# Attention stage: stack loads ahead of the sums' store, output weights split in four, dense last maxima, FP4 work at round ends

## The reference, cut to what matters

```python
x = x + attention(layernorm(x), Wqkv, bqkv, Wo, bo)   # x: 2 x 1024 x 512, 16 heads of 32
x = x + fp4_ffn(layernorm(x), ...)                    # weights packed as 4-bit codes
x = x + recurrence(layernorm(x), ...)
x = x + experts(layernorm(x), ...)

# attention, for batch b and head n
scores = einsum('bsnh,btnh->bnst', k, q) / sqrt(32)
scores = triu(scores) + -10000.0 * tril(ones, k=-1)
attn = softmax(scores, axis=2)
out = einsum('bnkq,bknh->bqnh', attn, v)
return out.reshape(b, s, 512) @ Wo + bo
```

## Time and profile before

| | |
|---|---|
| runs | 1803.70, 1817.19, 1809.32 us |
| median | 1809.32 us |
| span of the profiled execution | 1799.4 us |
| mean granted TensorE clock | 0.969 |
| PE busy | 1662.0 us (92%) |
| DVE busy | 1103.2 us (61%) |
| ACT busy | 703.2 us (39%) |
| POOL busy | 587.6 us (33%) |

### The profile page before, as it was taken

One profiled execution on the slowest core, in us unless ns is written; L12 is line 12 of the kernel. 1 busy time (PEld: TensorE's weight loads), 2 busy tenths in 40 slices (PEclk: granted clock), 3 DMA queues, 4 the chain that ended last, 5 costly groups with the idle time before them and its releaser, 6 DMA issues. The chain is left out here.

```text
span 1799.4 us, 22628 instructions
## 1 busy us (share of the span) xinstructions
PE 1662.0 (92%) x7201; PEld 1177.9 (65%) x7201; DVE 1103.2 (61%) x2382; ACT 703.2 (39%) x1330; POOL 587.6 (33%) x859
## 2 busy tenths in 40 slices
PE   6997899999989899999967999999699999999995
PEld 5886454555547677777755767677477777777774
DVE  5444766666736778787878567797544444444442
ACT  3211455555552455555442142212044334433442
POOL 3001333433551334444445051121133333333322
PEclk9998799999999999999988999999899999999998
DMA  7344456556623500000010031102799999999994
GB/s 253 115 141 134 139 159 156 160 161 162 164 70 108 188 1 1 1 1 1 1 59 33 0 119 51 47 21 72 254 325 354 338 357 351 345 345 350 353 354 91
DMA packets 120679, 284.83 MB, mean 158 GB/s; under 512 B 23472, under 2 KB 35248, under 8 KB 120304
## 3 DMA queue, kind: packets, MB, share of 16 engines
q1 hardware_dynamic: 106224, 247.71, 40.0%
q0 software_dynamic: 14336, 35.66, 9.0%
HBM read 224.03 MB, written 54.69 MB: 155 GB/s over the span
## 5 line engine op out<-in xcount | busy, mean ns | idle before, releaser
L897 ACT ACTIVATE probs<-bank 128x512 f32<-128x512 f32 (+3 forms) x384 | 167.6, 503 | 185.4 <-PE bank L840 183.9
L2000 POOL DMA_INDIRECT out_x<-e_y,row_out x64 | 104.0, 1626 | 316.4 <-DMA out_x<-e_y,row_out 174.1
L2035 PE MATMUL bank<-w_gate,xgt 128*128 128x352 f32 x512 | 163.7, 463 | 0.0
L2035 PE MATMUL bank<-w_up,xgt 128*128 128x352 f32 x512 | 161.9, 459 | 0.0
L2101 DVE TENSOR_TENSOR e_hidden<-e_silu,bank 128x352 f32<-128x352 f32 x64 | 33.4, 522 | 201.4 <-issue 181.6
L815 PE MATMUL bank<-k_stack,q_stack 96*128 96x512 f32 (+2 forms) x360 | 136.2, 391 | 22.2 <-DMA k_stack<-qk_parts 11.8
L1200 PE MATMUL bank<-ln_xt_hi,gu_codes 128*128 128x512 f32 x352 | 145.6, 414 | 10.8 <-DVE gate_sum L1273 5.3
L854 PE MATMUL bank<-probs,v_ones 128*64 128x512 f32 (+3 forms) x768 | 142.1, 506 | 6.7 <-POOL probs L764 6.7
L940 DVE CUSTOM_DVE_ANT_0 masked_scores<-bank,wide_mask 128x128 bf16<-128x128 f32 (+1 forms) x240 | 109.3, 482 | 63.5 <-PE bank L815 62.8
L840 PE MATMUL bank<-q_stack,k_stack 98*128 98x512 f32 (+3 forms) x384 | 141.0, 382 | 2.1 <-ACT probs L897 1.8
L764 POOL TENSOR_SCALAR_AFFINE_SELECT probs<-probs 128x128 f32<-128x128 f32 x256 | 77.9, 321 | 196.5 <-ACT probs L897 192.4
(11 more groups left out here) (261 smaller groups left out, 3842.2 us busy)
## 6 DMA issues: line engine op xcount, KB each, us to landing
w_gate<-in_w_gate SPq DMA_DIRECT2D x64, 704.0 KB, 6.7
w_up<-in_w_up SPq DMA_DIRECT2D x64, 704.0 KB, 7.8
w_down<-in_w_down SPq DMA_DIRECT2D x64, 512.0 KB, 8.7
q_stack<-qk_parts SPq DMA_DIRECT2D x96, 128.0 KB, 3.8
k_stack<-qk_parts SPq DMA_DIRECT2D x96, 128.0 KB, 4.0
w_down<-in_w_down SPq DMA_DIRECT2D x64, 192.0 KB, 10.0
qk_parts<-qk_stage_hi SPq DMA_DIRECT2D x32, 256.0 KB, 2.0
qk_parts<-qk_stage_lo SPq DMA_DIRECT2D x32, 256.0 KB, 2.3
```

The source lines that it names most:

```text
L897: act.activation(probs[u % PROBS][:, 0:cols], m.bank[EXPB[u % 3]][:, 0:cols], ACT.Exp, scale=scale).then_inc(exp_ready, 1)
L2000: pool.indirect_dma_start(out=a["out"][:, :], out_offset=bass.IndirectOffsetOnAxis(ap=row_out[e % YS][:, :], axis=0), in_=y[e % YS][:, :], ...
L2035: last = pe.matmul(m.bank[bank[e % 2]][:, 0:F], xt[e % 2][:, k, :], w[e % R][:, k, :], start=(k == 0), stop=(k == KT - 1))
```

## The change

Six edits, all in `attention_phase`:

1. SyncE's loop issues `store_inverse` and `spread_inverse` one pair later (p - 2 in place of p - 1), right behind the stack load, and no longer at the end of the iteration. Pair 14's come behind the loop.
2. GpSimd splits the output weights in four pieces of 128 x 512 (`split_wo`), two in pair 0 and two in pair 1, behind `place_v` and behind the masks of round 2. Who needs them waits for four pieces.
3. `maxima_at(p, n)` gives the full lists as before; for pair 14 one entry per unit for n below 12, and the rest (the turn) at n = 17.
4. ScalarE does the high part and the last output copy at the start of round 1, the codes at the start of round 2, the first output copy at the start of round 3.
5. VectorE does its FP4 steps behind the last unit of a round: gate-up words behind unit 5, low part behind unit 11, down words behind unit 17.
6. VectorE inverts the sums behind unit 23.

```diff
--- before.py
+++ after.py
@@ -608,6 +608,13 @@
                 first.append(("unit", q, i))
         return first
 
+    def maxima_at(p, n):
+
+        entries = maxima_of(p)
+        if p + 2 < PAIRS:
+            return entries[(U + 1) * n // U:(U + 1) * (n + 1) // U]
+        return entries[n:n + 1] if n < LEAD else entries[LEAD:] if n == TURN_AT else []
+
     place = {entry: i for i, entry in enumerate(entry for p in range(-1, PAIRS) for entry in maxima_of(p))}
     FIRST_DONE = 2 * TPC
     DIAGONAL = [n for n in range(U) if EXP_UNITS[n // 2][1] == EXP_UNITS[n // 2][0] * P]
@@ -701,7 +708,7 @@
             def spread_inverse(p):
                 sp.wait_ge(inverse_stored, 16 * (p + 1))
                 if p == 0:
-                    sp.wait_ge(wo_ready, 1)
+                    sp.wait_ge(wo_ready, KT)
                 need(sp, normalized, p // 2 - 1)
                 for j in range(2):
                     u = (2 * p + j) % 4
@@ -720,6 +727,9 @@
                 if p >= 1 and p + 2 < PAIRS:
                     sp.wait_ge(scored, U * p)
                     load(p + 2)
+                if p >= 2:
+                    store_inverse(p - 2)
+                    spread_inverse(p - 2)
                 if p >= 1:
                     dq.sync_store_down(sp, p - 1)
                     move_out(p - 1)
@@ -727,9 +737,8 @@
                     dq.sync_load_down(sp, p + 1)
                     place_max(p + 1)
                 dq.sync_store_gu(sp, p)
-                if p >= 1:
-                    store_inverse(p - 1)
-                    spread_inverse(p - 1)
+            store_inverse(PAIRS - 2)
+            spread_inverse(PAIRS - 2)
             move_out(PAIRS - 1)
             store_inverse(PAIRS - 1)
             spread_inverse(PAIRS - 1)
@@ -781,17 +790,23 @@
 
             pool.wait_ge(ones_set, 2 * SLOTS + 4)
             place_v(0)
-            pool.wait_ge(wo_loaded, 16)
-            pool.tensor_copy(wo_hi[:, :, :], wo_raw[:, :, :]).then_inc(wo_hi_ready, 1)
-            pool.wait_ge(wo_hi_ready, 1)
-            pool.tensor_tensor(wo_lo[:, :, :], wo_raw[:, :, :], wo_hi[:, :, :].bitcast(F32),
-                               ALU.subtract).then_inc(wo_ready, 1)
+            def split_wo(k):
+                pool.wait_ge(wo_loaded, 16)
+                pool.tensor_copy(wo_hi[:, k, :], wo_raw[:, k, :]).then_inc(wo_hi_ready, 1)
+                pool.wait_ge(wo_hi_ready, k + 1)
+                pool.tensor_tensor(wo_lo[:, k, :], wo_raw[:, k, :], wo_hi[:, k, :].bitcast(F32),
+                                   ALU.subtract).then_inc(wo_ready, 1)
+
             for p in range(PAIRS):
                 mask_round(p, 0)
                 mask_round(p, 1)
                 if p + 1 < PAIRS:
                     place_v(p + 1)
+                if p < 2:
+                    split_wo(2 * p)
                 mask_round(p, 2)
+                if p < 2:
+                    split_wo(2 * p + 1)
                 if p % 2 == 1 and p >= 3:
                     normalize((p - 3) // 2)
                 mask_round(p, 3)
@@ -865,19 +880,18 @@
                 exp_unit(0, n)
                 maxima(before[1 + LEAD // 2 + LEAD // 2 * n // EXP_ROUND:1 + LEAD // 2 + LEAD // 2 * (n + 1) // EXP_ROUND])
             for p in range(PAIRS):
-                ahead = maxima_of(p)
                 for r in range(ROUNDS):
                     for n in range(EXP_ROUND * r, EXP_ROUND * (r + 1)):
                         if p > 0 or r > 0:
                             exp_unit(p, n)
-                        maxima(ahead[len(ahead) * n // U:len(ahead) * (n + 1) // U])
+                        maxima(maxima_at(p, n))
                     if r >= 1:
                         value_round(p, r - 1)
                     elif p >= 1:
                         value_round(p - 1, ROUNDS - 1)
             value_round(PAIRS - 1, ROUNDS - 1)
 
-            pe.wait_ge(wo_ready, 1)
+            pe.wait_ge(wo_ready, KT)
             for t in range(NT):
                 pe.wait_ge(a_lo, t + 1)
                 need(pe, x_added, t - 2)
@@ -906,14 +920,13 @@
             for p in range(PAIRS):
                 for r in range(ROUNDS):
                     for n in range(EXP_ROUND):
-                        if n == 2 and r == 1 and p >= 1:
+                        if n == 0 and r == 1 and p >= 1:
+                            dq.scalar_hi(act, p - 1)
                             copy_out(p - 1, 1)
-                        if n == 2 and r == 3:
+                        if n == 0 and r == 2:
+                            dq.scalar_codes(act, p)
+                        if n == 0 and r == 3:
                             copy_out(p, 0)
-                        if n == 4 and r == 0 and p >= 1:
-                            dq.scalar_hi(act, p - 1)
-                        if n == 4 and r == 2:
-                            dq.scalar_codes(act, p)
                         exponential(p, EXP_ROUND * r + n)
             copy_out(PAIRS - 1, 1)
             for t in range(NT):
@@ -980,16 +993,15 @@
             maxima(maxima_of(-1))
             dq.vector_shifts(dve)
             for p in range(PAIRS):
-                ahead = maxima_of(p)
                 for n in range(U):
-                    maxima(ahead[len(ahead) * n // U:len(ahead) * (n + 1) // U])
-                    if n == 2:
+                    maxima(maxima_at(p, n))
+                    if n == EXP_ROUND - 1:
                         dq.vector_gu_bits(dve, p)
-                    if n == 6 and p >= 1:
+                    if n == 2 * EXP_ROUND - 1 and p >= 1:
                         dq.vector_lo(dve, p - 1)
-                    if n == 13:
+                    if n == 3 * EXP_ROUND - 1:
                         dq.vector_down_bits(dve, p)
-                    if n == 22 and p >= 1:
+                    if n == 4 * EXP_ROUND - 1 and p >= 1:
                         invert(p - 1)
 
             def split_attn(t):
```

## The result

Before has a median of 1810.68 us (4 runs), the changed kernel 1782.61 us (1771.64 to 1787.21, 4 runs): a ratio of 0.9845, 95% interval 0.9805 to 0.9885, so faster by 1.2 to 2.0%. The profiled execution of after is the fastest of its four.

The account below looks back on a forecast made before the run. TensorE's own work was taken to set the pace, other engines costing only its waits. Terms 6.7 + 6.8 + 4.0 + 4.0 = 21.5 us off the 1799.4 span, plus 9.9, gave 1787.8 us; own range 1781 to 1795.

Parts of the forecast that it names:

- The 9.9 us between span and median: Distance of the three runs' median, 1809.3 us, above the profiled span, 1799.4; assumed to stay the same after the change.
- The split: Pair 0: TensorE's whole wait for the masks behind GpSimd's output-weight split goes, 6.7 us, range 4.9 to 8.5.
- round ends: FP4 work moved to round ends: the low-part subtraction's 0.31 us per pair goes, 4.0 us over 13 pairs, bounds 0 and 8.
- that open question: Pair 0: whether the clock's next rise comes later or earlier against the work; up to about half of 3.72 us at stake.
- The stack loads: Loads ahead of the sums' store: the excess of pairs 4, 5, 10 and 11 goes, 6.84 us, bounds 3 and 8.
- there is no reserve: Old SyncE order: the stack's first product starts 3.8 us after the last load issue, while slower landings take 4.7.
- What pays for it: SyncE's queue: store and spread stand behind twelve loads, maxima's rows go out at 357.5 instead of 355.83; no stall taken.
- the store's landing hides behind the wait for the low parts: SyncE, mid-pair: free of landing and spread between 348.0 and 354.4, while low parts come about 352.9 anyway.
- The rival of the other side: Pair starts: maxima's rows come 3.4 us late in each of 13 pairs, 22.7 us lost, 1832; chance 0.05.
- The rival that round ends give nothing: Round ends: VectorE's work is only shifted and not caught up, so without the 4.0 us 1791.8; chance 0.15.
- Dense maxima: Pair 14: waits behind the unpacking and for the turn, and the low clock, go; 3.99 us, bounds 2 and 5.

Follow-up runs that it names:

- E2: Kernel before with only the output-weight split in four pieces; 1802.12 us, ratio 0.9981.
- E7: Changed kernel with the extra maxima entry of a full list taken at unit 17 instead of two products at unit 23; 1788.29 us, ratio 0.9871.
- E11: Changed kernel with SyncE's old order, sums' store and spread at the end of an iteration; 1805.49 us, ratio 0.9961.
- E5: Changed kernel with the low-part subtraction back behind unit 6 and the high part back at n = 4 of round 0; 1784.92 us, ratio 0.9851.
- E6: Changed kernel with the sums' store issued ahead of the stack loads, only its spread behind them; 1777.55 us, ratio 0.9819.
- E10: Changed kernel with the last 13 maxima again spread evenly over pair 14's units; 1786.09 us, ratio 0.9837.
- E9: Changed kernel with six extra 2 KB DMAs ahead of the rows of maxima in each pair; 1831.98 us, ratio 1.0129.
- E1: Kernel before with only the sums' store and spread moved one pair later, behind the stack loads; 1800.64 us, ratio 0.9959.
- E4: Kernel before with only ScalarE's and VectorE's FP4 work at round ends and the inversion behind unit 23; 1818.95 us, ratio 1.0042.
- E3: Kernel before with only pair 14's maxima one per unit and the turn at unit 17; 1805.28 us, ratio 0.9973.

## Why the prediction was right, and where it was not

The forecast was 1787.8 us and faster by over 1%; measured were 1782.6 and 1.55%. The sum of the terms was 21.5 us, the stage gave 27.8. Where the time goes was right in all four places; that the terms could be added was luck, since the working did not see which of them need each other.

The 9.9 us between span and median were read as what lies around the span. Every run on record whose span is listed is 1.7 to 1.8 us above its own span, so some 8 of the 9.9 say only that the profiled execution of before was that much shorter than the median run. After's span lies 12.7 below its median: this term is scatter and no constant.

**The split: right, 6.7 predicted, 6.9 measured (E2).** The predicted sign was there too: the first value products of after start at 189.70 (predicted about 192), without a wait. The first piece in after, GpSimd:

```profile
189.96 0.62 POOL L795 CAST wo_hi<-wo_raw 128x512 fp32r<-128x512 f32 x1 [2.62 <-DMA wo_raw<-in_wo]
190.66 1.27 POOL L797 TENSOR_TENSOR wo_lo<-wo_raw,wo_hi 128x512 fp32r<-128x512 f32 x1
```

The same copy in before:

```profile
191.76 1.89 POOL L785 CAST wo_hi<-wo_raw 128x2048 fp32r<-128x2048 f32 x1 [15.81 <-DMA wo_raw<-in_wo]
```

So the masks of before stood behind the arrival of the weights, for which GpSimd idled 15.81 us, and not only behind the split that the working names; the change takes the masks out from behind both. A piece takes 1.9 us (estimated under 2.2), and no mask behind one is waited for. Pair 0 gained 2.3 us more than this term. About 0.8 is the unpacking's move, which takes away a wait for a maximum (1.45 us in E2): E7 and E11 have that move, and like E2 a clock of 0.50 until 16 us into the pair, and their pair 0 takes 27.4 against E2's 28.2. It is a gain of the round ends in pair 0 that the prediction overlooked, since it took pair 7 for all pairs. The rest, 1.5, goes with the clock: in after, E5, E6 and E10 it was at 1.00 for one stretch of 3.4 us around 183 and rose for good at 191 to 193 (pair 0 25.8 to 25.9), in E7, E9 and E11 it stayed at 0.50 until 194 to 195 (26.5 to 27.4). The prediction named that open question (range 4.9 to 8.5); what makes the clock rise earlier in one kernel was not found out and stays open.

**The stack loads: right in size and cause (E1), wrong as a term that stands by itself.** 6.84 us of stalls were predicted to go, and all of them go. The step that failed is that the four terms were summed as if each kept its value whatever the others do. The working said of the old order "there is no reserve", and did not draw from it that the 0.31 us per pair of the next term needs the reserve, nor that the later inversion starts the chain later: E4 shows 4.0 predicted becoming a loss of some 8, E11 the same with everything else in. The sum was near only because all parts were applied. SyncE's queue of after across pair 8's start at 345.47 (against the earlier trace rows):

```profile
340.09 2.71 SPq L688 DMA_DIRECT2D q_stack<-neg_max_t  x4
...
343.80 1.39 SPq L250 DMA_DIRECT2D q_stack<-qk_parts  x3
...
349.41 0.42 SPq L706 DMA_DIRECT2D softmax_inverse<-sums_inverse  x1
353.64 0.77 SPq L715 DMA_DIRECT2D sums_inverse_rows<-softmax_inverse  x2
355.04 0.34 SPq L573 DMA_DIRECT2D fp_down<-fp_hi  x1
...
360.94 2.72 SPq L688 DMA_DIRECT2D q_stack<-neg_max_t  x4
```

The loads begin 1.7 us before the pair's first score (predicted about 3), and end 3.9 us into it. The first maxima product with that stack starts 9.5 us into the pair, so 5.6 us are left for the landing where before had 3.8.

**What pays for it: hidden, but by less than the working had it.** The sums' store was issued at 349.41 and the spread behind it at 353.64: it landed about 4.2 us later, where the same store took 1.4 before. The Trainium skill (DMA: Bandwidth & Descriptors, Queues, rings and completion order) says that a DMA's completion follows the earlier writes of its engines. That is what the trace shows: each of the twelve times that it stands behind loads in after, the small store lands 0.2 to 0.5 us after the last of them, and in E6, ahead of them, SyncE does not wait for it. The end of the spread came near the middle of its predicted span (8.9 us into the pair; 5.3 to 11.7 predicted), 0.6 us before the low parts let SyncE go on. So "the store's landing hides behind the wait for the low parts" held, by 0.4 us per pair. The four rows of maxima are issued 2.1 us before the next pair's first score (2.9 predicted), and no score waits for them.

**The rival of the other side was rightly left out of the sum, and priced too far away.** It was said to eat the gain from 1.65 us per pair on, with a chance of 0.05 since both worst cases would have to meet. E9 shows the path: 3.68 us into SyncE's queue cost 3.64 us in each pair. There is less than half a microsecond of reserve in the loop, and 2.1 us from the last issue's end to the score, of which the landing needs 1.2 (E9: issued by 372.97, score at 374.15). The working had counted the hidden landing as cover without working out what SyncE's whole round of waits and issues leaves per pair.

**Round ends: right in place, mis-sized: 0.31 predicted, 0.5 measured per pair (E5; 6.3 us over pairs 1 to 13 where 4.0 were predicted).** The 0.31 was one late product, the only one with a wait in the earlier trace rows. The two products behind it come late as well, since the one that had waited runs longer (0.50 us in place of 0.40) and its neighbours start 0.34 and 0.26 us apart in place of 0.23. The distance from the score product ahead of the stall (348.72 in the earlier trace rows) to the first value product is 1.58 us in before, against the 1.12 of after; read in the trace of before, it would have given the size. The rival that round ends give nothing falls.

**Dense maxima: right in size (3.99 predicted, 4.06 measured), and again a joint gain.** The working did count the unpacking's stall to this term, though it is edit 5 that removes it; alone, edit 3 gains nothing (E3) and leaving it out costs 5.7 us (E10). That 4.06 comes so near to 3.99 is partly luck: pair 14 of E2, which has the code of before, takes 24.61 where before took 23.08. There the clock fell to 0.50 for 3.4 us behind the 1.01 us wait for a maximum, and behind the same wait of before it did not.

By the Trainium skill (SBUF — State Buffer, Who interferes with whom) a VectorE and a GpSimd instruction can shut each other out. The traces agree at five places where the two met: 4.49, 3.32, 2.64 (E3), 2.59 (E7), 3.1 for three small ones (E10). What the working missed is that the joins at the end of pair 14 are such a place too: their 4.01 us wait would have stood there once the rest was moved, as E4 and E10 have it.

**Pair 15** gained 0.7 us, left out of the sum: its rounds 1 and 3 get shorter by 0.2 and 0.5 through the same moves.

Together: 6.7 + 6.8 + 4.0 + 4.0 became 6.9 (E2) + 7.1 (E1, pairs 1 to 12) + 6.3 (E5) + 4.1 in pair 14, with 2.3 more in pair 0, 0.7 in pair 15 and 0.4 in pairs 1 to 13 that no single run holds: 27.8.

## What to carry to other kernels

Before summing the parts of a change, ask of each which resource it uses the reserve of: a queue whose waits and issues form a loop has one number that counts, its length against the pair's, and a part that shortens the pair can be a loss as long as that loop sets the pace (E4). Size a stall by the distance between two fixed points around it, not by the recorded wait. Where two engines shut each other out, list all places at which they will meet after the move; one that is left keeps the whole price.

## What the hardware showed

A small store of 1.4 us to its landing took 3.8 to 5.1 when twelve 128 KB loads were issued ahead of it in the same queue, and SyncE did not wait for its landing when it was issued ahead of them (after, E6).

Waits of TensorE of 1 to 2.3 us were followed by a granted clock of 0.50 in some places: 2.08 us in E4's pair 7, then 6.8 us at half speed; 2.06 us at the earlier trace rows and 1.65 us at the earlier trace rows before; 1.01 us in E2's pair 14. In others they were not: 1.45 us in pair 10 and 1.01 us in pair 14 of before, 1.83 us in E4's pair 12, 2.23 us ahead of the first product with the output weights in after. What decides between them stays open. Of the 5.2 us by which E4's pair 7 exceeds its pair 1, 2.1 are wait.

VectorE instructions of 0.17 to 0.6 us took 0.8 to 4.5 us where GpSimd instructions on SBUF ran beside them (E3, E7, E10), three in a row each anew in E10.
